# V tiles of the cross-attention moved from ahead of the loop into slots 0 to 7, Wo split in slots 1 and 3, one context buffer

## The chip, the cores and the metric

The kernel runs on one core of a Trainium2 chip. The metric is the device time of one execution in microseconds. The core has TensorE (PE in the profile), VectorE (DVE), ScalarE (ACT), GpSimd (POOL) and SyncE (SP); each runs its own instructions in order, and they wait for each other through semaphores. DMAs are issued by an engine's queue (mostly SyncE's, some ScalarE's).

## The reference

Multi-head cross-attention of 16 batches with 512 query rows of 512 features against 77 context rows, 16 heads of 32 features, followed by a residual and a layer norm:

```python
Q = split_heads(query @ Wq + bq)          # query: (16, 512, 512)
K = split_heads(key @ Wk + bk)            # key = value = context: (16, 77, 512)
V = split_heads(value @ Wv + bv)
scores = jnp.einsum('bhqd,bhkd->bhqk', Q, K) / np.sqrt(D_K).astype(np.float32)
attn = jax.nn.softmax(scores, axis=-1)
ctx = jnp.einsum('bhqk,bhkd->bhqd', attn, V)
ctx = ctx.transpose(0, 2, 1, 3).reshape(B, S, D_MODEL)
out = ctx @ Wo + bo
return _layer_norm(out + query, ln_gamma, ln_beta)
```

## The kernel before

Products with a weight matrix are made of three matmuls each, because both operands are split into a high and a low part: high x high, high x low, low x high. A product over 512 features is thus 4 x 3 = 12 matmuls.

**Stage one, `project_context`.** The context of all batches is 1232 columns. For each chunk of 128 features ScalarE casts Wk and the context to their high parts and VectorE subtracts to get the low parts; the context is cut in two pieces, `cx1` (the first `V_FIRST * P` = 512 columns) and `cx2` (720 columns, which lie in the tail of the buffers `ch` and `cl` that the loop uses later for the context of the attention). TensorE makes K in 12 tiles (four chunks of output features, each cut at columns 0, 512, 872 and 1232), ScalarE and VectorE evict it as high and low part, and SyncE stores it to DRAM in four pairs of DMAs. Then TensorE makes the first four V tiles (128 context rows each, from `cx1`) in the banks `pvv`, VectorE adds bv, and SyncE stores them. SyncE's order is: the K stores, a wait for them to land, four loads of `kb` (K of batch 0 laid out for the maxima), then the V stores, each behind a wait for VectorE. All engines meet at the end of the stage.

**Stage two, `attend`.** A loop over 64 chunks (16 batches x 4 groups of four heads), one per slot; the first 16 slots and the last ones are written out, the rest is a hardware loop. Lags set which work of which chunk falls in a slot. In slot g TensorE does, in this order: the Q product of chunk g (`p_q`, 12 matmuls); in slots 0 to 5 one of the six remaining V tiles (`project_v` into `p_o`); from slot 4 on the values (`p_v`) and sums (`p_den`) of chunk g-4; from slot 3 on the first two score matmuls (`p_s`) of chunk g-3; and then four times a quarter of the output projection (from slot 8 on, `p_o`), a score matmul at two of these, and one `p_a` matmul, whose rows VectorE reduces to maxima. `p_a` has two banks, so the third and fourth wait for VectorE's first and second maxima. The score matmuls need `z`, which SyncE's queue puts together for a pair of slots: eight copies of the high part of Q, four of the low part, and four of the negated maxima (`z<-nmt`), in the second slot of a pair and at the start of the next.

VectorE does in slot g: the sums over keys of chunk g-4 (`sum_keys`), later slots' residual (`add_residual`), the low part of Q (`q_low`), the inverse of the sums and the division (`divide`, into one of two buffers of `cxt`), and the four maxima; in slots 0 to 5 the addition of bv to a V tile (`add_bv`) stands between the second and the third maximum. ScalarE then casts `cxt` to `ch`, and GpSimd subtracts to get `cl`.

Wo is split to `woh` and `wol` in slots 6 and 7; these lie where Wv's parts were, so the names `woh` and `wol` in rows of V tiles mean Wv. Its raw chunks lie in `xn` and in two buffers of `y`. The rows of gamma, beta and bo are loaded in slot 6.

Of the kernel before, what the change touches and what calls it, by code (L numbers as in the profile page):

```python
# [20 lines left out]
F32 = mybir.dt.float32  # L21
# [26 lines left out]
WO_SLOTS = (6, 7)  # L48

V_FIRST = 4  # L50
V_SLOTS = (0, 1, 2, 3, 4, 5)
# [37 lines left out]
def v_tiles(B, S2):  # L89

    return [(r, min(P, B * S2 - r)) for r in range(0, B * S2, P)]


def v_products(nc, keep, bank, parts, r, m):

    (cxh, cxl), wvh, wvl = parts, keep["wvh"], keep["wvl"]
    for kc in range(KC):
        for n, (x, w) in enumerate(((cxh, wvh), (cxh, wvl), (cxl, wvh))):
            last = nc.tensor.matmul(bank[0:m, :], x[:, kc, r:r + m], w[:, kc, :],  # L99
                                    start=(kc == 0 and n == 0), stop=(kc == KC - 1 and n == 2))  # L100
    return last


def project_context(nc, a, keep, kh_dram, kl_dram, v_dram, B, S2):
# [4 lines left out]
    cuts = [0, N1, N1 + (NK - N1) // 4 * 2, NK]  # L109
# [7 lines left out]
    with ExitStack() as ctx:  # L117
# [3 lines left out]
        def sem(name):  # L121
# [25 lines left out]
            (cx[:, kc % CX, N1:NK], cx2[0][:, kc, :], cx2[1][:, kc, :]))]  # L147
# [3 lines left out]
        with nc.Block() as block:  # L151
# [143 lines left out]
            @block.tensor  # L295
            def _(pe):
                def k_products(i, kc):
                    c, lo, hi = tiles_k[i]
                    (cxh, cxl), at = (cx1, lo) if hi <= N1 else (cx2, lo - N1)
                    for n, (w, x) in enumerate(((wkh, cxh), (wkh, cxl), (wkl, cxh))):  # L300
                        last = nc.tensor.matmul(pk[i % PK][:, 0:hi - lo], w[:, kc, P * c:P * (c + 1)],
                                                x[:, kc, at:at + hi - lo],
                                                start=(kc == 0 and n == 0), stop=(kc == KC - 1 and n == 2))
                    if kc == KC - 1:
                        last.then_inc(k_summed, 1)


                for kc in range(KC):
                    for i in range(PK):
                        if i < 2:  # L310
                            pe.wait_ge(kv_low, 3 * kc + 2 + i)
                        k_products(i, kc)
                for i in range(PK, 2 * PK):
                    pe.wait_ge(k_low_out, i - PK + 1)
                    for kc in range(KC):
                        k_products(i, kc)
                pe.wait_ge(kv_low, 4 * KC)
                for i, (r, m) in enumerate(tiles_v):
                    if i >= 2:
                        pe.wait_ge(v_out, i - 1)  # L320
                    v_products(nc, keep, pv[i % 2], cx1, r, m).then_inc(v_summed, 1)


def attend(nc, a, keep, kh_dram, kl_dram, v_dram, out, B, S, S2):
# [17 lines left out]
    assert VT <= V_FIRST + len(V_SLOTS) and max(V_SLOTS) < LAG_PV + 2  # L342
# [3 lines left out]
    with ExitStack() as ctx:  # L346
# [89 lines left out]
        def v_in_slot(g):  # L436

            if not isinstance(g.u, int):
                return []
            return [V_FIRST + n for n, k in enumerate(V_SLOTS[:VT - V_FIRST]) if k == PAIR * g.u + g.k]  # L440
# [8 lines left out]
        p_vp = p_o  # L449
        wo_raw = [xn[:, 0, :], xn[:, 1, :], y[:, 2, :], y[:, 3, :]]  # L450
# [18 lines left out]
        def _(sp):  # L469
# [56 lines left out]
            def slot(g):  # L526
# [20 lines left out]
                if g.back(WO_SLOTS[0] - 1).is_first():  # L547
                    load_wo(2)
                    load_wo(3)
# [19 lines left out]
        def _(pe):  # L569
# [97 lines left out]
            def project_v(i):  # L667

                pe.wait_ge(v_out, i)
                r, n = tiles_v[i]  # L670
                v_products(nc, keep, p_vp[:], keep["cx2"], r - V_FIRST * P, n).then_inc(v_summed, 1)

            def slot(g):
# [4 lines left out]
                for i in v_in_slot(g):  # L678
                    project_v(i)
# [26 lines left out]
        def _(act):  # L706
# [25 lines left out]
            def ctx_high(g):  # L732
                i = g.k // NCH % 2
                act.wait_ge(cx_ready, g.over(1, 1))
                if g.back(2).is_first():
                    act.wait_ge(v_summed, VT)
                if g.k % NCH == 0:
                    at_least(act, o_summed, g.over(NCH, -1, QT))
                nc.scalar.copy(ch[:, i, g.k % NCH, :], cx[:, g.k % 2, :]).then_inc(ch_ready, 1)  # L739
# [8 lines left out]
            def load_residual(m):  # L748

                if m.is_first():  # L750
                    act.wait_ge(wo_low, 2)
                    act.wait_ge(wo_high, 2)
# [29 lines left out]
            def split_wo_high(kc):  # L782
                act.wait_ge(wo_in[kc % 2], 16 * (kc // 2 + 1))
                act.wait_ge(v_summed, VT)
                nc.scalar.copy(keep["woh"][:, kc, :], wo_raw[kc]).then_inc(wo_high, 1)
# [3 lines left out]
            def slot(g):  # L789
# [30 lines left out]
                for i in v_in_slot(g):  # L820
                    store_v(i)
                if g.back(WO_SLOTS[0]).is_first():
# [33 lines left out]
        def _(dve):  # L856
# [6 lines left out]
            def add_residual(m):  # L863
# [3 lines left out]
                at_least(dve, stored[i], m.over(4, 0, 16))  # L867
                nc.vector.scalar_tensor_tensor(out=y[:, i, :], in0=p_o[:], scalar=0.0, in1=xn[:, m.k % 2, :],
# [56 lines left out]
            def add_bv(i):  # L925
# [4 lines left out]
                nc.vector.tensor_tensor(y[0:n, i % 4, :], p_vp[0:n, :], bv_row[0:n, :],  # L930
# [9 lines left out]
            def slot(g):  # L940
# [16 lines left out]
                if g.valid(NG):  # L957
                    for t in range(QT):
                        row_maxima(g, t)
                        if t == 1:  # L960
                            for i in v_in_slot(g):
                                add_bv(i)
# [69 lines left out]
        def _(pool):  # L1032
# [42 lines left out]
            def slot(g):  # L1075
# [56 lines left out]
def xattn(nc, a, out):  # L1132
# [5 lines left out]
    with ExitStack() as ctx:  # L1138

        keep = {n: ctx.enter_context(nc.sbuf_tensor(n, [P, KC, D], F32R)) for n in ("wqh", "wql", "woh", "wol")}  # L1140
# [46 lines left out]
```

## Time and profile before

| | us |
|---|---|
| median of 3 runs | 627.71 |
| lowest and highest run | 625.75, 628.01 |
| the profiled execution, its whole time | 627.87 |
| the profiled execution, span of the instructions | 626.0 |

| engine | busy us in the span |
|---|---|
| TensorE | 598.1 |
| VectorE | 496.7 |
| GpSimd | 444.9 |
| ScalarE | 363.6 |

The span is what the trace shows, from the first to the last instruction; the profiled execution's own time is 1.87 us more. Times in rows are counted from the span's start. Slot 0 begins at 48.75 us, slot 9 at 121.01 us. Matmuls are pipelined: the busy time of one is longer than the distance from its start to the next one's start, and the distance is what a stream of them costs.

### The profile page before, as it was taken

The page shows a single profiled execution, that of the slowest core. Times are in us where ns is not written, and L with a number is a line of the kernel's source. Part 1 is how long each engine was busy: PE and PEld are TensorE (multiplying, and loading weights), DVE is VectorE, ACT ScalarE, POOL GpSimd, SP SyncE. Part 2 cuts the span into 40 slices and gives each one's busy share as a digit, 9 for nine tenths or more (in the row PEclk, how much of TensorE's full clock was granted, in tenths as well). Part 3 has the DMA queues.
Part 4 walks back from the last instruction along what each step waited for, and adds up shares of the span by engine and source line. Part 5 has one row for each costly group of instructions (what it writes and reads, how often), then busy time and mean ns, then how long its engine had stood idle before and what let it go on. Part 6 is the DMA issues. An engine that isn't in the chain of part 4 may idle for free.

```text
span 626.0 us, 12033 instructions
## 1 busy us (share of the span) xinstructions
PE 598.1 (96%) x3336; PEld 432.3 (69%) x3336; DVE 496.7 (79%) x912; ACT 363.6 (58%) x675; POOL 444.9 (71%) x396
## 2 busy tenths in 40 slices
PE   5998999999999999999999999999999999999793
PEld 5986765677777777777777777777777777776362
DVE  5423478888888888888888988888888888888575
ACT  5621235566666666666666666666666666656362
POOL 1335024648888888888888888888888888878676
PEclk9999999999999999999999999999999999999797
DMA  8757778988979898989898979989797989796413
GB/s 313 292 225 190 193 183 222 205 186 200 231 197 228 212 223 209 206 218 218 211 216 207 231 201 219 219 202 245 177 241 198 231 204 233 190 225 169 122 52 134
DMA packets 93392, 129.58 MB, mean 207 GB/s; under 512 B 49936, under 2 KB 49936, under 8 KB 93360
## 3 DMA queue, kind: packets, MB, share of 16 engines
q1 hardware_dynamic: 74544, 94.94, 60.9%
q10 hardware_dynamic: 18816, 34.25, 21.3%
q8 instruction: 15, 0.25, 0.2%
q14 instruction: 17, 0.14, 0.1%
HBM read 53.94 MB, written 24.35 MB: 125 GB/s over the span
## 4 chain that ended last, share of the span: by engine, by line
PE 83%; POOL 2%; DVE 2%; SPq 2%; issue 1%; ACT 1%; DMA 0%; POOLq 0%; ACTq 0%; DVEq 0%
PE p_q L579 29%; PE p_o L645 25%; PE p_s L609 10%; PE p_v L620 10%; PE p_a L595 6%; PE p_o L99 3%; SPq L523 1%; DVE nm L921 1%; PE p_den L628 1%; DMA z<-nmt 0%; DVE rden L886 0%; ACT prob L714 0%; POOL cl L1062 0%; POOL xt L1104 0%; POOL y L1053 0%
## 5 line engine op out<-in xcount | busy, mean ns | idle before, releaser
L714 ACT ACTIVATE prob<-p_s 77x512 f32<-77x512 f32 x256 | 143.2, 591 | 108.2 <-PE p_s L609 93.0
L1062 POOL TENSOR_TENSOR cl<-cxt,ch 128x512 fp32r<-128x512 f32 x64 | 83.1, 1298 | 115.0 <-ACT ch L739 115.0
L921 DVE TENSOR_REDUCE nm<-p_a 128x4 f32<-128x308 f32 x256 | 115.9, 475 | 49.3 <-PE p_a L595 48.1
L876 DVE TRANSPOSE_TENSOR_REDUCE part<-prob 96x64 f32<-96x2048 f32 x64 | 146.4, 2287 | 2.4 <-issue 1.3
L729 ACT ACTIVATE qh<-p_q,bq_col 128x512 fp32r<-128x512 f32 x64 | 44.0, 687 | 125.0 <-PE p_q L579 125.0
L579 PE MATMUL p_q<-xh,wqh 128*128 128x512 f32 x256 | 101.1, 395 | 1.7 <-PEq L151 1.7
L579 PE MATMUL p_q<-xl,wqh 128*128 128x512 f32 x256 | 101.3, 396 | 0.0
L579 PE MATMUL p_q<-xh,wql 128*128 128x512 f32 x256 | 101.0, 395 | 0.0
L609 PE MATMUL p_s<-z,ks 97*77 97x512 f32 x256 | 95.8, 415 | 5.2 <-DMA z<-nmt 3.7
L645 PE MATMUL p_o<-woh,ch 128*128 128x512 f32 x240 | 96.0, 400 | 0.8 <-issue 0.7
L645 PE MATMUL p_o<-wol,ch 128*128 128x512 f32 x240 | 95.1, 396 | 0.0
L645 PE MATMUL p_o<-woh,cl 128*128 128x512 f32 x240 | 94.6, 394 | 0.0
L1043 POOL TENSOR_TENSOR xl<-xt,xh 128x512 fp32r<-128x512 f32 x60 | 77.2, 1287 | 20.0 <-ACT xh L721 19.9
L595 PE MATMUL p_a<-kb,qh 128*128 128x308 f32 x256 | 79.1, 312 | 2.9 <-DVE nm L921 2.8
L1057 POOL TENSOR_TENSOR y<-y,beta_row 128x512 f32<-128x512 f32 x58 | 75.2, 1297 | 4.5
L1069 POOL TENSOR_TENSOR xn<-xn,bo_row 128x512 f32<-128x512 f32 x60 | 77.3, 1289 | 0.0
L1053 POOL TENSOR_TENSOR y<-y,gamma_row 128x512 f32<-128x512 f32 x58 | 74.4, 1283 | 0.0
L620 PE MATMUL p_v<-prob,vb 77*32 77x512 f32 x512 | 69.1, 612 | 0.0
L595 PEld LDWEIGHTS p_a<-kb,qh 128*128 128x128 f32 x256 | 48.3, 189 | 22.9 <-DVE nm L921 7.6
L913 DVE SCALAR_TENSOR_TENSOR ql<-p_q,bq_col,qh 128x512 fp32r<-128x512 f32 x64 | 47.9, 748 | 17.0 <-ACT qh L729 13.5
L645 PEld LDWEIGHTS p_o<-woh,ch 128*128 128x128 f32 x240 | 45.6, 190 | 18.2 <-issue 5.5
L579 PEld LDWEIGHTS p_q<-xh,wqh 128*128 128x128 f32 x256 | 48.1, 188 | 13.2 <-issue 2.1
(127 smaller groups left out, 934.4 us busy)
## 6 DMA issues: line engine op xcount, KB each, us to landing
z<-qh SPq DMA_DIRECT2D x256, 128.0 KB, 3.7
z<-ql SPq DMA_DIRECT2D x128, 128.0 KB, 4.8
xn<-in_x ACTq DMA_DIRECT2D x60, 256.0 KB, 3.3
out_dram<-y SPq DMA_DIRECT2D x60, 256.0 KB, 4.3
xt<-in_x_t ACTq DMA_DIRECT2D x58, 256.0 KB, 4.9
ks<-k_high SPq DMA_DIRECT2D x32, 154.0 KB, 4.7
cx<-in_ctx_t SPq DMA_DIRECT2D x4, 616.0 KB, 5.6
k_high<-kth SPq DMA_DIRECT2D x4, 616.0 KB, 3.4
```

Source lines behind the costliest of these rows:

```text
L579: last = nc.tensor.matmul(p_q[:], w[:, kc, P * c:P * (c + 1)], x[:, i, kc, :], start=(kc == 0 and n == 0), stop=(kc == KC - 1 and n == 2))
L595: nc.tensor.matmul(p_a[t % 2][:, 0:HC * S2], qh[:, g.k // 2 % 2, g.k % 2, P * t:P * (t + 1)], kb[g.k // NCH % 2][:, g.k % NCH, :], start=T ...
L609: nc.tensor.matmul(p_s[j % 2][0:S2, :], ks[0:KR, g.k // NCH % 2, h, :], z[0:KR, i, j, g.k % 2, :], start=True, stop=True).then_inc(s_summe ...
L620: nc.tensor.matmul(p_v[DK * j:DK * (j + 1), :], vb[0:S2, g.k // NCH % 2, DK * h:DK * (h + 1)], prob[0:S2, j, :], start=True, stop=True)
L645: last = nc.tensor.matmul(p_o[:], x[:, i, kc, P * t:P * (t + 1)], w[:, kc, :], start=(kc == 0 and n == 0), stop=(kc == KC - 1 and n == 2))
L714: nc.scalar.activation(prob[0:S2, j, :], p_s[j % 2][0:S2, :], ACT.Exp, scale=SCALE).then_inc(prob_ready, 1)
L876: nc.vector.tensor_reduce(part[:], prob[0:KP, :, :].rearrange("p h (i r) -> p (h i) r", r=DK), AX_X, ALU.add, apply_transpose=True).then_i ...
L921: nc.vector.tensor_reduce(nm[:, t, g.k % 2:HALF:2], p_a[t % 2][:, 0:HC * S2].rearrange("p (h k) -> p h k", k=S2), AX_X, ALU.max, negate=Tr ...
L1043: nc.gpsimd.tensor_tensor(xl[:, i, n.k % KC, :], xt[:, n.k % 2, :], xh[:, i, n.k % KC, :].bitcast(F32), ALU.subtract).then_inc(xl_ready, 1)
L1057: nc.gpsimd.tensor_tensor(rows(m), rows(m), beta[:], ALU.add).then_inc(y_done, 1)
L1062: nc.gpsimd.tensor_tensor(cl[:, i, g.k % NCH, :], cx[:, g.k % 2, :], ch[:, i, g.k % NCH, :].bitcast(F32), ALU.subtract).then_inc(cl_ready, 1)
L1069: nc.gpsimd.tensor_tensor(xn[:, m.k % 2, :], xn[:, m.k % 2, :], bo[:], ALU.add).then_inc(xb_ready, 1)
```

## The change

Ahead of the loop there are two V tiles instead of four (`V_FIRST`). The other 976 context rows are cut into eight tiles of 122 rows, one for each of the slots 0 to 7, and their 12 matmuls are no longer in one piece behind the Q product: a quarter (three matmuls) stands ahead of each `p_a` matmul, as the output projection does from slot 8 on. The sums over keys therefore stand right behind the Q product. The addition of bv moves to the next slot, ahead of `q_low` on VectorE, and so does the V tile's store on ScalarE's queue. The second piece of the context, now 976 columns, lies tile by tile (8 x 4 x 122) instead of chunk by chunk, so the K matmuls on it read four runs of 122 columns; K is cut at columns 0, 256, 744 and 1232. Wv's parts have buffers of their own, so Wo can be split early, in slots 1 and 3, through `xn` alone; SyncE's queue waits for the first half's split before it loads the second. The rows of gamma, beta and bo are loaded in slot 5. `cxt` has one buffer, so a division waits until the last one's result is split. Two unused buffers go, and the scratch for dynamic DMAs is made smaller.

```diff
-WO_SLOTS = (6, 7)
+WO_SLOTS = (1, 3)
+ROWS_SLOT = 5
-V_FIRST = 4
-V_SLOTS = (0, 1, 2, 3, 4, 5)
+V_FIRST = 2
+V_LATE = 8
...
-    return [(r, min(P, B * S2 - r)) for r in range(0, B * S2, P)]
+    first = V_FIRST * P
+    width = (B * S2 - first) // V_LATE
+    return [(P * i, P) for i in range(V_FIRST)] + [(first + width * k, width) for k in range(V_LATE)]
...
-    cuts = [0, N1, N1 + (NK - N1) // 4 * 2, NK]
+    cuts = [0, N1, (N1 + NK) // 2, NK]
...
-            (cx[:, kc % CX, N1:NK], cx2[0][:, kc, :], cx2[1][:, kc, :]))]
+            (cx[:, kc % CX, N1:NK].rearrange("p (k n) -> p k n", k=V_LATE), cx2[0][:, :, kc, :], cx2[1][:, :, kc, :]))]
...
-                    (cxh, cxl), at = (cx1, lo) if hi <= N1 else (cx2, lo - N1)
+                    bank = pk[i % PK][:, 0:hi - lo]
+                    if hi <= N1:
+                        cxh, cxl = (t[:, kc, :] for t in cx1)
+                    else:
+                        half = V_LATE // 2
+                        k = half * (lo > N1)
+                        cxh, cxl = (t[:, k:k + half, kc, :] for t in cx2)
+                        bank = bank.rearrange("p (k n) -> p k n", k=half)
...
                 if kc >= 2:
-                    sp.wait_ge(v_stored[kc], 32)
-                sp.dma_start(wo_raw[kc], a["Wo"][P * kc:P * (kc + 1), :]).then_inc(wo_in[kc % 2], 16)
+                    sp.wait_ge(wo_high, kc - 1)
+                    sp.wait_ge(wo_low, kc - 1)
+                sp.dma_start(xn[:, kc % 2, :], a["Wo"][P * kc:P * (kc + 1), :]).then_inc(wo_in[kc % 2], 16)
...
-                for i in v_in_slot(g):
-                    project_v(i)
                 if v.valid(NG) and g.valid(NG):
                     values(v)
                     sums(v)
...
                     if o.valid(NS):
                         project_out(o, kc)
+                    for i in v_in_slot(g):
+                        project_v(i, kc)
                     if s.valid(NG) and g.valid(NG) and kc in (1, 2):
                         scores(s, kc + 1)
...
-                at_least(dve, ch_ready, g.over(1, -1))
-                at_least(dve, cl_ready, g.over(1, -1))
-                nc.vector.tensor_tensor(cx[:, i, :], p_v[:], rden[:], ALU.mult).then_inc(cx_ready, 1)
+                at_least(dve, ch_ready, g.over(1))
+                at_least(dve, cl_ready, g.over(1))
+                nc.vector.tensor_tensor(cx[:], p_v[:], rden[:], ALU.mult).then_inc(cx_ready, 1)
...
+                for i in v_in_slot(g.back(1)):
+                    add_bv(i)
                 if m.valid(NS) and g.valid(NG):
                     add_residual(m)
...
-                        if t == 1:
-                            for i in v_in_slot(g):
-                                add_bv(i)
...
-        keep["wvh"], keep["wvl"] = keep["woh"], keep["wol"]
...
-    nc = bacc.Bacc("TRN2", target_bir_lowering=False, num_devices=1)
+    nc = bacc.Bacc("TRN2", target_bir_lowering=False, num_devices=1, dynamic_dma_scratch_size=2048)
```

On TensorE, at the end of slot 0, before (`p_o` rows are V matmuls, `p_a` rows feed the maxima, `p_q` rows are the Q product):

```order
L99 MATMUL p_o<-woh,ch 128x512
L99 MATMUL p_o<-wol,ch 128x512
L99 MATMUL p_o<-woh,cl 128x512
L595 MATMUL p_a<-kb,qh 128x308 x4
L579 MATMUL p_q<-xh,wqh 128x512
```

The same engine in slot 0 of the changed kernel, from the end of the Q product:

```order
L587 MATMUL p_q<-xh,wql 128x512
L102 MATMUL p_o<-wvh,ch 122x512
L102 MATMUL p_o<-wvl,ch 122x512
L102 MATMUL p_o<-wvh,cl 122x512
L603 MATMUL p_a<-kb,qh 128x308
L102 MATMUL p_o<-wvh,ch 122x512
```

The four `p_a` stood together behind the whole V tile; now each stands behind a quarter of it.

On TensorE in slot 4, before, from the last V matmul on, with what each waits for (`p_v` the values, `p_den` the sums, `p_s` the scores):

```order
L99 MATMUL p_o<-woh,cl 128x512
L620 MATMUL p_v<-prob,vb 32x512 [waits vb_in0,prob_ready]
L620 MATMUL p_v<-prob,vb 32x512 x3
L628 MATMUL p_den<-part,sel 32x16 [waits part_ready]
L628 MATMUL p_den<-part,sel 32x16 x3
L609 MATMUL p_s<-z,ks 77x512 [waits prob_ready,mx_in0,z_in0]
```

The same place in the changed kernel, from the last matmul of the Q product on:

```order
L587 MATMUL p_q<-xh,wql 128x512
L628 MATMUL p_v<-prob,vb 32x512 [waits vb_in0,prob_ready]
L628 MATMUL p_v<-prob,vb 32x512 x3
L636 MATMUL p_den<-part,sel 32x16 [waits part_ready]
L636 MATMUL p_den<-part,sel 32x16 x3
L617 MATMUL p_s<-z,ks 77x512 [waits prob_ready,mx_in0,z_in0]
L617 MATMUL p_s<-z,ks 77x512 [waits prob_ready]
L102 MATMUL p_o<-wvh,ch 122x512 [waits v_out]
```

The V tile stood ahead of the sums, and now stands behind the first two score matmuls; it waits for the bank `p_o` (`v_out`), which VectorE frees in the same slot.

On SyncE's queue, around slot 2, before (`z` for slots 0 and 1, then V of batch 0, then `z` for slots 2 and 3):

```order
L523 DMA z<-ql 32x1024 x3
L518 DMA z<-nmt 1x32x32 [waits max_turned]
L518 DMA z<-nmt 1x32x32 x3
L493 DMA vb<-v_all 77x512 [waits v_stored0]
L523 DMA z<-qh 32x1024 [waits qh_ready]
```

The same place in the changed kernel:

```order
L531 DMA z<-ql 32x1024 x3
L526 DMA z<-nmt 1x32x32 [waits max_turned]
L526 DMA z<-nmt 1x32x32 x3
L500 DMA vb<-v_all 77x512 [waits v_stored0]
L515 DMA xn<-in_Wo 128x512 [waits wo_low,wo_high] x2
L531 DMA z<-qh 32x1024 [waits qh_ready]
```

The second half of Wo, with its wait for ScalarE and GpSimd, now stands ahead of the `z` copies of slots 2 and 3.

## Rows read from the trace of the kernel before

**Rows 1.** The page, chain that ended last: share of the span by engine

```profile
PE 83%; POOL 2%; DVE 2%; SPq 2%; issue 1%; ACT 1%; DMA 0%; POOLq 0%; ACTq 0%; DVEq 0%
```

**Rows 2.** Windows, slots 0, 3, 4, 6, 9: length, busy per engine, granted clock, DMA

```profile
core 0: us, PE busy (x) PEld busy (x) DVE busy (x) ACT busy (x) POOL busy (x), PEclk, DMA share, GB/s
48.75:55.91 7.16, 6.72 (x28) 5.22 (x29) 1.98 (x5) 1.72 (x3) 6.96 (x5) 1.00 0.99 237
...
70.07:78.14 8.07, 7.68 (x33) 5.57 (x33) 3.08 (x7) 2.68 (x5) 0.00 (x0) 1.00 0.54 137
78.14:87.82 9.68, 9.14 (x49) 5.98 (x49) 7.05 (x12) 3.76 (x8) 1.29 (x1) 1.00 0.78 188
...
97.46:104.64 7.18, 6.34 (x38) 3.72 (x37) 6.84 (x12) 4.16 (x9) 2.55 (x2) 1.00 0.82 216
...
121.01:129.29 8.28, 8.28 (x50) 6.01 (x49) 7.00 (x12) 4.69 (x10) 3.79 (x3) 1.00 1.02 188
```

**Rows 3.** Timeline of slot 0: start, duration, engine, instruction, idle before and releaser

```profile
51.63 0.39 PE L99 MATMUL p_o<-woh,ch 128*128 128x512 f32 x1
...
51.88 0.69 ACT L729 ACTIVATE qh<-p_q,bq_col 128x512 fp32r<-128x512 f32 x1 [14.38 <-PE p_q L579]
...
54.41 0.45 PE L595 MATMUL p_a<-kb,qh 128*128 128x308 f32 x2
...
55.28 0.80 PE L595 MATMUL p_a<-kb,qh 128*128 128x308 f32 x2 [0.43 <-DVE nm L921]
```

**Rows 4.** Timeline of SyncE's queue at the end of stage one

```profile
37.56 0.43 SPq L184 DMA_DIRECT2D k_low<-ktl  x1
41.63 1.77 SPq L193 DMA_DIRECT2D kb<-k_high  x4
43.44 0.90 SPq L197 DMA_DIRECT2D v_all<-y  x2
...
47.83 0.33 SPq L197 DMA_DIRECT2D v_all<-y  x1
```

**Rows 5.** Timeline of TensorE: first V matmul of stage one, first matmul of stage two

```profile
35.71 0.40 PE L99 MATMUL pvv<-woh,cx1h 128*128 128x512 f32 x1
...
48.75 0.47 PE L579 MATMUL p_q<-xh,wqh 128*128 128x512 f32 x1 [1.69 <-PEq L151]
```

**Rows 6.** Timeline of TensorE: two K matmuls of 360 columns

```profile
31.76 0.33 PE L301 MATMUL pk<-ch,wkh 128*128 128x360 f32 x1
31.93 0.33 PE L301 MATMUL pk<-cl,wkh 128*128 128x360 f32 x1
```

**Rows 7.** Timeline of the first context chunk's casts and its second subtraction

```profile
5.00 0.62 ACT L203 CAST cx1h<-cx 128x512 fp32r<-128x512 f32 x1 [0.96 <-DMA cx<-in_ctx_t]
5.53 0.79 ACT L203 CAST ch<-cx 128x720 fp32r<-128x720 f32 x1
...
6.35 0.91 DVE L244 TENSOR_TENSOR cl<-cx,ch 128x720 fp32r<-128x720 f32 x1
```

**Rows 8.** Windows in the tail, columns as in rows 2

```profile
587.00:591.00 4.00, 4.00 (x13) 1.41 (x13) 1.70 (x2) 0.00 (x0) 3.92 (x4) 0.50 0.00 0
591.00:592.00 1.00, 1.00 (x4) 0.69 (x3) 0.00 (x0) 0.00 (x0) 0.71 (x1) 0.55 0.65 246
```

**Rows 9.** Timeline of TensorE in the tail: the first matmuls after a gap

```profile
586.77 1.11 PE L609 MATMUL p_s<-z,ks 97*77 97x512 f32 x2 [3.69 <-DMA z<-nmt]
```

**Rows 10.** Timeline of SyncE's queue: z for slots 0 and 1

```profile
59.62 5.42 SPq L523 DMA_DIRECT2D z<-qh  x8
...
67.63 3.20 SPq L518 DMA_DIRECT2D z<-nmt  x4
```

**Rows 11.** Tile z, 50 to 110 us: from issue to landing

```profile
DMA to landing us min/median/max: 2.3/3.3/4.7
```

**Rows 12.** Timeline in the tail: GpSimd's subtraction and VectorE's next division

```profile
603.94 1.28 POOL L1062 TENSOR_TENSOR cl<-cxt,ch 128x512 fp32r<-128x512 f32 x1 [1.78 <-ACT ch L739]
...
608.07 0.69 DVE L906 TENSOR_TENSOR cxt<-p_v,rden 128x512 f32<-128x512 f32 x1
```

More of the change, by code:

```diff
@@ L89, in v_tiles, with v_products @@
 def v_tiles(B, S2):
-    return [(r, min(P, B * S2 - r)) for r in range(0, B * S2, P)]
[L94 to L100, printed above, removed]
+    first = V_FIRST * P
+    width = (B * S2 - first) // V_LATE
+    assert width <= P and first + V_LATE * width == B * S2
+    return [(P * i, P) for i in range(V_FIRST)] + [(first + width * k, width) for k in range(V_LATE)]
+def v_products(nc, keep, bank, cxh, cxl, kc, m):
+    wvh, wvl = keep["wvh"], keep["wvl"]
+    for n, (x, w) in enumerate(((cxh, wvh), (cxh, wvl), (cxl, wvh))):
+        last = nc.tensor.matmul(bank[0:m, :], x, w[:, kc, :],
+                                start=(kc == 0 and n == 0), stop=(kc == KC - 1 and n == 2))
     return last
@@ L320, in _ @@
                         pe.wait_ge(v_out, i - 1)
-                    v_products(nc, keep, pv[i % 2], cx1, r, m).then_inc(v_summed, 1)
+                    for kc in range(KC):
+                        cxh, cxl = (t[:, kc, r:r + m] for t in cx1)
+                        last = v_products(nc, keep, pv[i % 2], cxh, cxl, kc, m)
+                    last.then_inc(v_summed, 1)
 def attend(nc, a, keep, kh_dram, kl_dram, v_dram, out, B, S, S2):
@@ L439, in v_in_slot @@
                 return []
-            return [V_FIRST + n for n, k in enumerate(V_SLOTS[:VT - V_FIRST]) if k == PAIR * g.u + g.k]
+            return [V_FIRST + n for n in range(V_LATE) if n == PAIR * g.u + g.k]
         def wo_in_slot(g):
@@ L546, in slot @@
                     store(g.back(LAG_STORE))
-                if g.back(WO_SLOTS[0] - 1).is_first():
+                if g.back(WO_SLOTS[0] + 1).is_first():
                     load_wo(2)
@@ L665, in project_last, with project_v @@
                         last.then_inc(o_summed, 1)
[L667 to L671, printed above, removed]
+            def project_v(i, kc):
+                if kc == 0:
+                    pe.wait_ge(v_out, i)
+                m = tiles_v[i][1]
+                cxh, cxl = (t[:, i - V_FIRST, kc, :] for t in keep["cx2"])
+                last = v_products(nc, keep, p_o, cxh, cxl, kc, m)
+                if kc == KC - 1:
+                    last.then_inc(v_summed, 1)
             def slot(g):
@@ L734, in ctx_high @@
                 act.wait_ge(cx_ready, g.over(1, 1))
-                if g.back(2).is_first():
-                    act.wait_ge(v_summed, VT)
+                if isinstance(g.u, int) and PAIR * g.u + g.k < V_LATE:
+                    act.wait_ge(v_summed, V_FIRST + PAIR * g.u + g.k + 1)
                 if g.k % NCH == 0:
                     at_least(act, o_summed, g.over(NCH, -1, QT))
-                nc.scalar.copy(ch[:, i, g.k % NCH, :], cx[:, g.k % 2, :]).then_inc(ch_ready, 1)
+                nc.scalar.copy(ch[:, i, g.k % NCH, :], cx[:]).then_inc(ch_ready, 1)
             def square(m):
@@ L750, in load_residual @@
                 if m.is_first():
[L751 to L752 removed]
+                    act.wait_ge(wo_low, KC)
+                    act.wait_ge(wo_high, KC)
                 all_at_least(act, (squared, m.over(1, -1)))
@@ L867, in add_residual @@
                 at_least(dve, stored[i], m.over(4, 0, 16))
+                if isinstance(m.u, int) and PAIR * m.u + m.k < 4:
+                    dve.wait_ge(v_stored[i], 16 * len(tiles_v[i::4]))
                 nc.vector.scalar_tensor_tensor(out=y[:, i, :], in0=p_o[:], scalar=0.0, in1=xn[:, m.k % 2, :],
@@ L947, in slot @@
                     minus_mean_over_std(g.back(LAG_NORMALIZE))
+                for i in v_in_slot(g.back(1)):
+                    add_bv(i)
                 if m.valid(NS) and g.valid(NG):
@@ L1149, in xattn @@
             keep[n] = ctx.enter_context(nc.sbuf_tensor(n, shape, dt))
-        keep["wvh"], keep["wvl"] = keep["woh"], keep["wol"]
         n2, part = B * S2 - V_FIRST * P, 2 * KC * S
-        assert KC * n2 <= part - 2 * S
+        assert KC * n2 <= part
         for n in ("ch", "cl"):
@@ L1156, in xattn @@
             keep[n] = buffer[:].rearrange("p (b c s) -> p b c s", b=2, c=KC)
-            keep.setdefault("cx2", []).append(buffer[:, part - KC * n2:part].rearrange("p (c n) -> p c n", c=KC))
+            late = buffer[:, part - KC * n2:part]
+            keep.setdefault("cx2", []).append(late.rearrange("p (k c n) -> p k c n", k=V_LATE, c=KC))
         for n in ("bq_in", "xh_ready", "xl_ready", "kb0_zeroed", "v_summed", "v_out"):
```

24 lines of the change are left out of this document (8 added, 16 removed).

## The prediction

> **What bounds the kernel now.** I read the chain of work that ended last first: TensorE (PE) carries 83% of it [rows 1], so what counts is when TensorE works, and whether it works without a break. The windows by slot come next, since the change touches slots 0 to 8 and the stage ahead of them [rows 2]. The reader is to see three kinds of slot. From slot 9 on TensorE is busy for all of its 8.28 us. Slot 0 takes 7.16 us with 0.44 idle, and slots 0 to 2 have 21.3 together (48.75 to 70.07). Slot 4 takes 9.68, with 0.54 idle and VectorE busy for 7.05, and slot 5 the same (87.82 to 97.46); both have a V tile ahead of the sums that VectorE's chain waits for. Slot 6, which has no V tile, takes 7.18, of which VectorE works 6.84. From the first row's 48.75 to the last row's 121.01 slots 0 to 8 take 72.26 us. Last I read the seam between the two stages: SyncE's queue and TensorE around 36 to 49 us [rows 4, 5].
>
> **Two V tiles fewer ahead of the loop.** A V tile is 12 matmuls, 2.78 us (51.63 to 54.41) [rows 3], so two tiles less are 5.6 us of TensorE. Not all of that comes off, because SyncE's queue is next late. Before, it sends the last K rows at 37.56, waits until they have landed, sends the four kb loads from 41.63, two V stores from 43.44 for 0.90, and the last V store at 47.83, for which it had waited [rows 4]; the loop's first matmul stands 0.59 after that store's end (48.16 to 48.75) [rows 4, 5]. With two stores the queue is through at 44.34, and slot 0 starts at 44.93 if K ends as before. K ends a little later, for two reasons. The context is cut at 256 instead of 512 columns, so the second piece has 976 instead of 720: VectorE's subtraction of it, 0.91 us before, becomes about 1.23 [rows 7], and TensorE's first tile is half as long and no longer covers it. That is worth between 0 and 0.9 (the whole row); I take 0.4. And the last K tile has 488 instead of 360 columns: at the casts' slope (0.62 for 512, 0.79 for 720 columns) and VectorE's 0.91 for 720 [rows 7] its two evictions grow by 0.10 and 0.16. Slot 0 starts at 44.93 + 0.40 + 0.25 = 45.6: **3.2 us** gained.
>
> **The K matmuls** themselves have as many columns as before. Spacing is 0.23 for 512 (2.78 / 12 [rows 3]) and 0.17 for 360 [rows 6], so it falls with the columns, and 256 would be 0.12. No row shows a matmul so short behind a 128-column weight load; if the load could not go under the 0.17 that the rows show, 48 of them would cost 48 x 0.045 = 2.1 us. I take 0, as the spacing shows no floor yet. The Trainium skill (TensorE: Matmul & The Clock Gate, section LDWEIGHTS) has a weight load take its columns at 1.2 GHz, an estimate of 107 ns for 128 columns: by that the term is 0 too, by the row's bound 2.1; no row here shows the load alone.
>
> **The idle seam.** TensorE has its last V matmul out at 35.71 + 0.4 + 24 x 0.233 = 41.7 and drained 0.17 later (0.40 less 0.23) [rows 5], and waits until 45.6: 3.7 us instead of 1.69. The trace has both. After 1.69 the granted clock is 1.00 and the first 12 matmuls take 2.88 (48.75 to 51.63), full spacing [rows 2, 3, 5]. In the tail a gap of 3.69 ends at 586.77 [rows 9]; the granted clock behind it is 0.50 (1.2 of 2.4 GHz) from 587 to 591 and has a mean of 0.55 in 591 to 592 [rows 8], so it is back at 591.9: 5.1 us of work at half speed, which loses up to 2.5 us. So the price is between 0 and 2.5. I take **1.7**: the gap is as long as the tail's, but dense matmuls stand before and after it, where the tail's were broken. The Trainium skill (the same page, section Why this matters for your kernels) warns that idle gaps between bursts of matmuls throw the clock back; by that rule the sum is the one below, by the row of 1.69 it is 1.7 less, and the tail's gap agrees with the rule.
>
> **Slots 0 to 2** have the V tile in four parts between the four p_a matmuls, instead of ahead of them. p_a needs qh, ready at 51.88 + 0.69 = 52.57, 0.94 after the Q product's stream ends at 51.63 [rows 3]; the first 0.70 of V covers most of that, and about 0.35 stays. The wait of 0.43 for VectorE's maxima [rows 3] goes, since 0.70 of V lies between any two p_a. A slot is 2.80 + 2.78 + 0.35 + 4 x 0.15 = 6.53; three with a slow first matmul 19.7 against 21.3.
>
> **Slot 3** is where part of it goes back. Its score matmuls stand ahead of V now and need z, which SyncE's queue fills: it starts at 59.62, 3.7 after slot 1's beginning (48.75 + 7.16 = 55.91 [rows 2]), and its last copy goes out at about 70.1, 10.5 later [rows 10]; landing is 2.3 to 4.7, median 3.3 [rows 11]. Counted from slot 0's start, now: 6.6 + 3.7 + 10.5 + 3.3 = 24.1, while the Q product ends at 19.7 + 2.8 = 22.5. So a wait of 1.6 (0.6 to 3.0) that V hid before, and a slot of 2.80 + 1.6 + 4 scores of 0.23 + 2.78 + 0.6 = 8.7 instead of 8.07 [rows 2].
>
> **Slots 4 to 8** each have the work of slot 9: a V tile is as many matmuls as an output projection, and VectorE's addition of bv takes the place of the residual's. The sums stand right behind the Q product in slots 4 and 5, so VectorE's chain no longer starts a V tile late. I take 8.28 for each [rows 2]. Slots 4 and 5 gain 1.4 each, slot 6 pays 1.1 for its new tile, and 7 and 8 together (104.64 to 121.01 before) pay 0.2. In all 19.7 + 8.7 + 5 x 8.28 = 69.8 against 72.26: **2.5 us** gained.
>
> **Edits at nothing.** One context buffer: VectorE's next division now waits for GpSimd's subtraction; the tightest place is the tail, where it ended at 603.94 + 1.28 = 605.22 and the division began at 608.07 [rows 12], 2.85 to spare; gone, it would delay the maxima behind it on VectorE, and TensorE's p_a with them. Wo in slots 1 and 3: four ScalarE casts (0.62 for this width [rows 7]) and four GpSimd subtractions (1.28 [rows 12]) move to slots in which both engines have most of their time free [rows 2]; SyncE's wait for the first two stands behind the z copies and the V load of slot 2, ahead of slot 3's z, which cannot go before slot 3's qh anyway. If that cover fails, slot 3's z is late by as much, but it is not needed until slot 5. The row constants go out a slot sooner on ScalarE's queue, the extra weight buffers cost memory only, and the smaller scratch belongs to no queue that the trace shows.
>
> **Sum.** The profiled execution took 627.87 (span 626.0), 0.16 above the median of 627.71. 627.87 - 3.2 - 2.5 + 1.7 = **623.9**.
>
> **Rivals.** (a) The clock holds over the seam, as it did over 1.69: 622.2. For it: the work around is dense; against: the tail. (b) z lands late in slot 3: 4.7 instead of 3.3 makes the wait 3.0, close to the tail's gap, so that the clock may fall a second time: 623.9 + 1.4 = 625.3, and with 2.5 more 627.8; half of that gives 626.6. For it: the stores of V and the loads of x share these microseconds; against: the median landing. (c) Slower than before: the K matmuls on the second context piece now read four separate runs of 122 columns instead of 360 in a row. There are 96, all ahead of the seam, so that every delay is the total's. From 4.0 / 96 = 0.042 us each, a fifth of their 0.22 (0.23 x 488 / 512), the gain is gone; at 0.08 each, 7.7 in all, the time is 631.6. No row shows such a read, and none shows a cost for one; the K stage has no other cover. (d) That the two tiles leave the stage and it does not end sooner is priced above: 3.2 instead of 5.6.
>
> **How the numbers follow.** The forecast has a chance of 0.47, (a) 0.25, (b) 0.20, (c) 0.08. A measurement of this kernel tells about 0.5%, 3.1 us, from no change, so faster ends at 624.6. All of (a) and 0.33 of the forecast lie below: faster 0.58; the rest of the forecast and (b) make 0.34; slower is (c). The range goes from (a) with an early landing, 622.2 - 0.9 = 621.3, to (b)'s upper end, 627.8.
>
> **What would show it.** The first Q product at 45.6, not 48.75, after an idle gap of 3.7; a granted clock of 0.5 behind it, or the Q product at full spacing if (a); slots 0 to 2 at 6.5 at full clock; in slot 3 a wait for z of about 1.6; slots 4 to 8 at 8.3. I am wrong if the stage ahead of the loop ends later than 46.5, if a slot from 4 to 8 takes over 8.6, or if a slot after 9 differs from 8.28.

## The result, and the profile after

The changed kernel is slower: 639.73 us (637.77 to 640.92) against 627.27 (625.75 to 628.01), a ratio of 1.0208 with an interval of 1.0187 to 1.0229. The prediction was 623.9, with a range that ended at 627.8. The profiled execution took 640.92, its span 639.1, which is 13.1 more than before. The chain that ended last, as in [rows 1]:

```profile
PE 80%; DMA 4%; SPq 4%; POOL 2%; issue 1%; ACT 1%; DVE 0%; POOLq 0%; ACTq 0%; DVEq 0%
```

DMA had 0% before and has 4% now.

Windows of the changed kernel by slot, columns as in [rows 2]: slots 0, 1, 3, slots 4 to 8 together, slot 9.

```profile
core 0: us, PE busy (x) PEld busy (x) DVE busy (x) ACT busy (x) POOL busy (x), PEclk, DMA share, GB/s
46.17:54.33 8.16, 8.03 (x28) 6.17 (x29) 2.16 (x5) 1.72 (x3) 7.03 (x5) 0.79 1.05 243
54.33:60.83 6.50, 6.41 (x31) 4.95 (x29) 3.17 (x6) 2.23 (x4) 2.62 (x3) 1.00 0.41 100
67.31:84.73 17.42, 10.13 (x34) 7.58 (x33) 3.27 (x6) 3.17 (x6) 0.00 (x0) 0.71 0.79 173
84.73:126.17 41.44, 41.44 (x242) 29.86 (x241) 35.29 (x53) 20.40 (x37) 13.99 (x11) 1.00 0.77 189
126.17:142.60 16.43, 11.21 (x50) 7.92 (x49) 7.03 (x12) 4.94 (x10) 5.02 (x4) 0.79 0.84 187
```

Two slots stick out. Slot 3 takes 17.42 where 8.7 was forecast (8.07 before [rows 2]), and slot 9, which the change was not to touch, 16.43 instead of 8.28. Slots 4 to 8 take 41.44, that is 8.29 each, slot 1 6.50: as forecast. What TensorE waited for from slot 0 to slot 10 (columns: total, times, longest):

```profile
PE p_s L617 <- DMA z<-nmt: 7.3, 1, 7.3
PE p_o L653 <- DVE y L881: 5.0, 1, 5.0
PE p_q L587 <- PEq L154: 3.8, 1, 3.8
```

Three waits, one in each of slots 3, 9 and 0. The last is the seam that the prediction spoke of. **Slot 9's wait**, followed back in the chain of work that ended last (start, duration, what), and VectorE's timeline there:

```profile
118.01 17.15 DMA v_all<-y
...
135.29 0.15 DVE y L881
```

```profile
135.29 0.69 DVE L881 SCALAR_TENSOR_TENSOR y<-p_o,xn 128x512 f32<-128x512 f32 x1 [6.23 <-DMA v_all<-y]
```

The store of slot 6's V tile, the last but one, went out at 118.01 and landed 17.15 us later. VectorE's residual (`add_residual`, L880) has a new wait for that store, because its result goes into the same buffer of `y`; the description of the change does not name this wait. VectorE stood 6.23 us, and TensorE 5.02 behind it.

**Slot 3's wait** is for `z`. SyncE's queue for slots 0 and 1, as in [rows 10], and from issue to landing for tile z, 50 to 110 us, as in [rows 11]:

```profile
58.05 8.63 SPq L531 DMA_DIRECT2D z<-qh  x8
...
70.27 3.03 SPq L526 DMA_DIRECT2D z<-nmt  x4
```

```profile
DMA to landing us min/median/max: 2.8/5.0/8.1
```

The same eight copies took 8.63 us to issue instead of 5.42, and landing took up to 8.1 instead of 4.7 (for the copies of Q; the view gives no landing of `z<-nmt`). Nothing in the change touches these copies. Both slots pay twice, since TensorE's clock fell behind each wait; windows of the changed kernel in slot 0, slot 3 and slot 9:

```profile
47.00:49.00 2.00, 2.00 (x6) 1.57 (x5) 0.00 (x0) 0.00 (x0) 1.94 (x2) 0.50 0.87 276
78.00:82.00 4.00, 4.00 (x12) 3.06 (x11) 0.48 (x1) 1.13 (x3) 0.00 (x0) 0.50 1.04 171
135.00:140.00 5.00, 3.95 (x10) 3.21 (x11) 3.42 (x9) 1.12 (x3) 1.28 (x1) 0.51 0.97 238
```

The granted clock (the column ahead of the DMA share) is 0.50 or 0.51, the lower level of 1.2 instead of 2.4 GHz, in all three. Set the two slots to what was forecast for them, and the profile gives 640.92 - (17.42 - 8.7) - (16.43 - 8.28) = 624.05. So the rest of the sum held, and the question is why a V store takes 17 us and z's copies are late.

### The profile page after: what moved, and what is told of

Same layout as the page of the kernel before. It is cut to its first block, busy times and chain, and to the rows that moved or that the text cites. A ratio compares the mean times of both kernels' runs of the same rounds, so it can differ in the third digit from the quotient of the medians.

```text
span 639.1 us, 12041 instructions
## 1 busy us (share of the span) xinstructions
PE 601.9 (94%) x3336; PEld 436.7 (68%) x3336; DVE 497.9 (78%) x912; ACT 364.6 (57%) x675; POOL 444.6 (70%) x396
## 4 chain that ended last, share of the span: by engine, by line
PE 80%; DMA 4%; SPq 4%; POOL 2%; issue 1%; ACT 1%; DVE 0%; POOLq 0%; ACTq 0%; DVEq 0%
PE p_q L587 27%; PE p_o L653 25%; PE p_s L617 10%; PE p_v L628 9%; PE p_a L603 5%; SPq L531 3%; DMA v_all<-y 3%; PE p_o L102 3%; DMA z<-nmt 1%; SPq L526 1%; PE p_den L636 1%; POOL cl L1074 0%; POOL y L1065 0%; POOL xt L1116 0%; ACT prob L726 0%
## 5 line engine op out<-in xcount | busy, mean ns | idle before, releaser
L934 DVE TENSOR_REDUCE nm<-p_a 128x4 f32<-128x308 f32 x256 | 117.4, 476 | 62.8 <-PE p_a L603 61.8
```

The source lines that it names most:

```text
L934: nc.vector.tensor_reduce(nm[:, t, g.k % 2:HALF:2], p_a[t % 2][:, 0:HC * S2].rearrange("p (h k) -> p h k", k=S2), AX_X, ALU.max, negate=Tr ...
```

## The experiments

The theory (A) was the shape of the store: 122 rows instead of 128. The rivals were (B) that the V stores, now in the same microseconds as z's copies, crowd them out whatever their shape, and (C) that the loads of the row constants, which went out at 101.4 to 102.6 ahead of the last stores on ScalarE's queue, hold them back.

**e1: the same bytes in other pieces.** Each late V tile is stored as 112 and 10 rows; the semaphore counts follow.

```diff
-                act.dma_start(v_dram...[r:r + n, :], y[0:n, i % 4, :]).then_inc(v_stored[i % 4], 16)
+                for lo, hi in ((0, 112), (112, 122)):
+                    act.dma_start(v_dram...[r + lo:r + hi, :], y[lo:hi, i % 4, :]).then_inc(v_stored[i % 4], 16)
```

> The changed kernel with each store of a late V tile sent as two DMAs, of 112 and of 10 rows, instead of one of 122. Theory A: a DMA of 122 rows is spread over few of the 16 DMA engines, so it lands late (17 us in the trace) and whatever else goes through those engines queues behind it. Then slot 3's wait for z falls from 7.3 to about 1.6 us, slot 9's wait for the V store goes, slots 3 and 9 take 8.7 and 8.3, and the time is about 624. Rival B: the shorter slots 0 to 2 crowd the transfers of V, x, Wo and z into less time. Bytes and times are unchanged here, so both waits stay and the time is 638 to 641. Rival C: the V stores wait behind the three row loads on ScalarE's queue, moved to slot 5. Then slot 9's wait stays, some 6 us with a fall of the clock behind it, and only slot 3 could change.

Measured: 624.64 (ten runs, 622.94 to 626.14) against 626.47, ratio 0.9964 (0.9949 to 0.9979). TensorE's waits over the same stretch, SyncE's queue for slots 0 and 1, and the windows of slots 0 and 3:

```profile
PE p_q L593 <- PEq L160: 3.8, 1, 3.8
PE p_s L623 <- DMA z<-nmt: 1.0, 1, 1.0
PE p_s L623 <- issue: 0.3, 1, 0.3
```

```profile
58.16 5.64 SPq L537 DMA_DIRECT2D z<-qh  x8
```

```profile
45.40:54.44 9.04, 9.04 (x28) 7.07 (x29) 2.13 (x5) 1.72 (x3) 6.99 (x5) 0.67 0.93 219
67.42:75.72 8.30, 7.25 (x34) 5.55 (x33) 3.26 (x6) 3.14 (x6) 0.00 (x0) 1.00 0.70 175
```

The wait for the store is gone, z's first eight copies take 5.64 to issue, slot 3 takes 8.30 and slot 9 8.28. The bytes, the queue and the moment are the same, with one DMA more, so (B) and (C) fall. Landing of z's copies of Q over the whole stretch is hardly shorter, though:

```profile
DMA to landing us min/median/max: 2.6/4.4/7.5
```

So the 8.1 above is no mark of the 122 rows; it belongs to a copy that went out at 103.67, long after slot 3's. What slot 3 waits for is the last `z<-nmt` copy of slots 0 and 1. The trace also keeps the times at which a DMA steps its semaphore, its sign of landing, which the views do not print. By these steps that copy went out at 72.62 and landed at 77.31 in the changed kernel, and at 69.34 and 71.18 here: 3.3 later out and 2.9 longer under way.

**e2: is it the splitting or the row count?** Two pieces again, of 61 rows each: `((0, 61), (61, 122))` in e1's line.

> The same with two DMAs of 61 and 61 rows: as many DMAs as with 112 and 10, the same bytes. Theory A, if it is the number of rows that decides how many engines share a DMA: 61 has no divisor up to 16, so the stores land no sooner than with 122 rows and perhaps twice as late; the waits in slots 3 and 9 are 7 us or more each and the time is 640 or above, up to 670. If it was only that one DMA was split in two, the time is that of 112 and 10 rows, about 624. Rivals B and C: 638 to 641, as for one DMA.

Measured: 673.48 in one execution. One store on ScalarE's queue, the second piece of a tile, and TensorE's waits from 45 to 200 us:

```profile
65.43 7.33 ACTq L798 DMA_DIRECT2D v_all<-y  x1
```

```profile
PE p_a L609 <- ACT qh L747: 21.5, 3, 12.2
PE p_o L659 <- DVE y L888: 11.6, 2, 6.4
PE p_s L623 <- DMA z<-nmt: 4.0, 1, 4.0
PE p_q L593 <- PEq L160: 3.8, 1, 3.8
```

Smaller pieces are not the cure. That store keeps the queue for 7.33 us, so that ScalarE comes late to `qh`; with the stores of later tiles, TensorE waits 21.5 for `qh` in all. Bytes and number of DMAs are those of e1, so what counts is the number of rows in a piece. The Trainium skill (DMA: Bandwidth & Descriptors, section Why a DMA increments its semaphore by 16 and not by 1, on how many engines) says that a transfer is given to as many of the 16 DMA engines as the largest number up to 16 that divides its rows: 16 for 112 or 128, 10 for 10, but 2 for 122 and 1 for 61, always the first ones. The trace agrees on how many. A store of 128 rows steps its semaphore 16 times as it lands (kernel before). Each store of 122 rows steps it twice, besides one step at its issue (at 133.31 and 135.16 for the one that slot 9 waited for), and each of 61 rows once; the two pieces of e1 together make 16 and 10. No row shows which engines worked. By the last steps, the stores of the loop landed in 9.7 to 18.0 us in the changed kernel, in 4.0 to 8.0 in e1 (both pieces) and in 2.2 to 4.4 before.

**e9: one such store with nothing beside it.** The kernel before, with the last output rows of all stored as 122 and 6 rows.

```diff
-                sp.dma_start(out_dram[NS + t], x_last[t]).then_inc(stored[t], 16)
+                for lo, hi in (((0, 122), (122, P)) if t == 1 else ((0, P),)):
+                    sp.dma_start(out_dram[NS + t][lo:hi, :], x_last[t][lo:hi, :]).then_inc(stored[t], 16)
```

> The kernel before, where the very last store of the output (128 rows of 512) is sent as 122 and 6 rows; nothing else is on the queues by then, and the kernel ends when it has landed. Theory A: a store of 122 rows is slow by itself; the time rises by what it lands later, 6 to 14 us. If it was slow only because it stood behind others: no more than 1 us.

Measured: 633.19 (two runs), ratio 1.0110 (1.0077 to 1.0142), span 631.5. The last store on SyncE's queue, before and then here:

```profile
623.54 0.33 SPq L564 DMA_DIRECT2D out_dram<-xt  x1
```

```profile
623.26 0.69 SPq L565 DMA_DIRECT2D out_dram<-xt  x2
```

Before, the span ends 2.5 us after that row begins (626.0 - 623.5); here 8.2 (631.5 - 623.3). So a 122-row store is 5.7 us slower with nothing beside it but the other 6 rows, a little under the 6 to 14 expected. Windows with stores of 128 rows before, and behind the 122 rows here, columns as in [rows 2]:

```profile
622.00:624.00 2.00, 0.00 (x0) 0.00 (x0) 1.03 (x2) 0.00 (x0) 0.79 (x1) 0.50 1.01 378
```

```profile
626.00:630.00 4.00, 0.00 (x0) 0.00 (x0) 0.00 (x0) 0.00 (x0) 0.00 (x0) 0.50 0.12 44
```

The mean busy share of the 16 DMA engines is 0.12, what two busy ones of 16 give (0.125), and they move 44 GB/s instead of 378. So few engines are the cause of the slow store, as theory A has it. The 17.15 of the changed kernel is twice its 8.2; what adds the rest was not separated.

**e3: the shape alone in the kernel before.** The five loop tiles of 128 rows are stored as 122 and 6 rows, in the old order of work.

```diff
+    return ((0, 122), (122, n)) if i >= V_FIRST and n == P else ((0, n),)
...
-                act.dma_start(v_dram...[r:r + n, :], y[0:n, i % 4, :]).then_inc(v_stored[i % 4], 16)
+                for lo, hi in v_pieces(i, n):
+                    act.dma_start(v_dram...[r + lo:r + hi, :], y[lo:hi, i % 4, :]).then_inc(v_stored[i % 4], 16)
```

> The kernel before, where only the five stores of 128 rows in slots 0 to 4 are cut into 122 and 6 rows. Theory A: the V stores land in over 10 us instead of 2 to 4, the z copies of slots 0 to 3 are held up, TensorE waits for z in slot 3 or 5, and the time rises by 3 to 12 us. Rival B: the slots are as long as before, so nothing changes but one more DMA to issue per slot: 626 to 628.5.

Measured: 630.36 (629.55 to 636.22), ratio 1.0078 (1.0047 to 1.0108). TensorE's longest wait for scores (in slot 7), the clock behind it, and ScalarE's queue:

```profile
PE p_s L619 <- issue: 2.6, 1, 2.6
```

```profile
114.00:115.00 1.00, 1.00 (x4) 0.61 (x3) 0.80 (x2) 0.91 (x3) 0.00 (x0) 0.50 0.90 188
```

```profile
69.96 3.23 ACTq L790 DMA_DIRECT2D v_all<-y  x2
78.76 5.32 ACTq L790 DMA_DIRECT2D v_all<-y  x2
```

The stores of 122 and 6 rows landed in 9.3 to 17.8 us by their semaphore steps, as expected. The view names no releaser for the wait of 2.6, but it was for z, too: the last step of `z<-nmt` came at 111.73, 0.07 before the weight load of these scores (111.80). Behind it the granted clock fell to 0.50. The cost is 4.9 us (0.0078 x 626), not the 16.9 that slots 3 and 9 of the changed kernel had over their forecast. In the old order V stands ahead of the scores and covers z in slot 3, and `add_residual` does not wait for a store; but there are also five such stores here instead of eight. That 122 rows need the new order of work to cost what they did is likely, not shown.

**e4: the seam.** e1, with 14 matmuls whose result nobody reads between the last V tile of stage one and the loop.

```diff
                     last.then_inc(v_summed, 1)
+                pe.wait_ge(v_out, 1)
+                r, m = tiles_v[1]
+                for again in range(14):
+                    nc.tensor.matmul(pv[0][0:m, :], cx1[0][:, again % KC, r:r + m], wvh[:, again % KC, :], start=True, stop=True)
```

> The changed kernel with stores of 112 and 10 rows, and 14 matmuls behind the last V tile of stage one whose result nothing reads: they fill the seam ahead of the loop, in which TensorE was idle for 3.8 us. If it is the idle time that brings the clock down: the first Q product takes 2.8 to 2.9 us instead of 4.6 to 5.5, slot 0 6.6, and the time falls by 1.6 to 2.5, to about 622.5. If the slow start belongs to the start of a stage, whatever TensorE did before: slot 0 stays at 8 to 9 us and the time at 624.6.

Measured: 622.14 (620.66 to 624.10) against 626.04, ratio 0.9935 (0.9914 to 0.9955). The loop's first matmul, and the windows of slots 0, 3 and 4 (slot 5 is like slot 4):

```profile
45.64 0.47 PE L598 MATMUL p_q<-xh,wqh 128*128 128x512 f32 x1 [0.61 <-PEq L160]
```

```profile
45.64:52.30 6.66, 6.51 (x28) 5.03 (x29) 2.16 (x5) 1.72 (x3) 6.46 (x5) 1.00 1.06 268
65.29:73.83 8.54, 7.25 (x35) 5.54 (x33) 3.26 (x6) 3.14 (x6) 0.00 (x0) 1.00 0.70 181
73.83:82.11 8.28, 8.28 (x51) 5.96 (x49) 7.14 (x11) 4.59 (x9) 3.79 (x3) 1.00 0.99 212
```

The gap is 0.61 instead of 3.8, the clock stays at 1.00, and slot 0 takes 6.66 instead of 8.16 (changed kernel) or 9.04 (e1): the idle time was the cause of the low clock. This version has the lowest median here, ahead of both kernels.

**e6: slot 3 without its wait.** e4, with two quarters of V and their `p_a` ahead of the first scores in slot 3.

```diff
+                ahead = 2 if s.is_first() else 0
+                for kc in range(ahead):
+                    for i in v_in_slot(g):
+                        project_v(i, kc)
+                    rowmax_scores(g, kc)
                 if s.valid(NG):
                     scores(s, 0)
```

> The same, and in slot 3 alone the first two quarters of the V tile, each with its p_a matmul, stand ahead of the first score matmuls, which wait for z. If the wait of 1.1 us for z that is left in slot 3 is one that a V tile can hide, as it did before: slot 3 takes 7.2 to 7.5 instead of 8.3 and the time falls by another 0.8 to 1.1, to about 621.5. If VectorE's maxima, which now come sooner, or z itself only shift the wait: no difference, 622.5.

Measured: 622.86 (620.33 to 624.38) against 626.04, ratio 0.9941 (0.9924 to 0.9959), no gain over e4. The windows of slots 3 to 5, and ScalarE in slots 3 and 4:

```profile
65.69:73.81 8.12, 7.58 (x34) 5.50 (x33) 3.17 (x6) 3.14 (x6) 0.00 (x0) 1.00 0.61 162
73.81:83.33 9.52, 8.80 (x51) 5.81 (x49) 7.12 (x11) 5.25 (x10) 4.12 (x4) 1.00 1.03 189
83.33:92.18 8.85, 8.34 (x50) 5.96 (x49) 6.97 (x10) 3.33 (x7) 2.27 (x2) 1.00 1.07 237
```

```profile
77.74 0.62 ACT L814 CAST woh<-xn 128x512 fp32r<-128x512 f32 x1 [1.19 <-DMA xn<-in_Wo]
...
78.71 0.69 ACT L758 ACTIVATE qh<-p_q,bq_col 128x512 fp32r<-128x512 f32 x1 [0.34 <-issue]
```

Slot 3 gained 0.42, but slots 4 and 5 lost 1.8. ScalarE waited for Wo's second half to land, and `qh` of slot 4 came behind it. That made Wo's casts the suspect.

**e10: Wo's second half one slot later.** e6 with `WO_SLOTS = (1, 4)` for `(1, 3)`.

> The version with warm matmuls and slot 3's early maxima, and one number more: Wo's second half is cast in slot 4 instead of slot 3. In the run before, ScalarE waited 1.81 and 1.19 us in slot 3 for Wo's second half to land, the second cast began at 77.74, and qh of slot 4 came only at 78.71; slot 4 took 9.52 and slot 5 8.85 instead of 8.28 to 8.30 each. Theory (these casts hold up qh, and through it slots 4 and 5): no cast waits in slot 3, slots 4 and 5 together take 16.6 to 17.2 instead of 18.37, and the profiled time falls by 1.2 to 1.8 against the version before, to about 621 (ratio to the kernel before 0.990 to 0.993). Rival (slots 4 and 5 are long because slot 3 is short: z or VectorE's chain is late whatever ScalarE does): slots 4 and 5 together stay at 18.0 to 18.5 and the time at 622.9.

Measured: 624.06 (620.48 to 625.90) against 627.24, ratio 0.9945 (0.9921 to 0.9969). Windows of slots 3 to 5, and TensorE's wait in slot 5:

```profile
66.14:74.26 8.12, 7.58 (x35) 5.50 (x34) 3.17 (x6) 3.15 (x6) 0.00 (x0) 1.00 0.63 173
74.26:82.53 8.27, 8.27 (x50) 5.96 (x49) 7.14 (x11) 3.44 (x7) 1.30 (x1) 1.00 1.05 221
82.53:92.61 10.08, 8.35 (x51) 5.97 (x49) 7.02 (x10) 5.05 (x10) 5.01 (x4) 1.00 1.09 193
```

```profile
88.27 0.66 PE L628 MATMUL p_s<-z,ks 97*77 97x512 f32 x2 [1.73 <-issue]
```

The theory was half right. Slot 4 is back to 8.27, so the casts had held it up; but slot 5 now takes 10.08, and slots 4 and 5 together 18.35, as the rival had it. Slot 5's first scores need z of slots 2 and 3, whose last copies went out at 81.9. The row names no releaser, but the semaphore of `z<-nmt` made its last step at 88.18, 0.06 before the weight load of these scores (88.24). In e6 it was 87.75 and 87.81; in e4 the last step came at 85.41, TensorE at 86.04, and there was no wait. So it is z that holds slot 5. SyncE's queue began those copies 24.5 us after slot 0 here and 24.4 in e4 (70.98 - 46.49, 70.04 - 45.64), so they do not move when slot 3 gets shorter, and slot 5 meets them.

**e7: V in one piece.** e1 with each late V tile whole behind the Q product, as the kernel before had it.

```diff
+                for i in v_in_slot(g):
+                    for kc in range(KC):
+                        project_v(i, kc)
...
-                    for i in v_in_slot(g):
-                        project_v(i, kc)
```

> The changed kernel with stores of 112 and 10 rows, but each late V tile in one piece right behind the Q product, as before. If the gain of the slots comes from the V matmuls among the maxima and behind the sums: slots 0 to 2 go back to 7.1, slots 4 to 7 to 9.6 each, slot 3 loses its wait for z; 3 x 0.6 + 4 x 1.35 - 1.1 = 6 us more, about 630.5. If only the matmuls' number counts: 624.6.

Measured: 633.67 in one execution. Of TensorE's waits from 45 to 150 us, those for VectorE:

```profile
PE p_o L108 <- DVE y L951: 2.9, 4, 0.9
PE p_a L609 <- DVE nm L942: 2.3, 7, 0.4
```

Slots 1 and 2 take 7.11 and 7.12 instead of 6.50, and slots 4 to 7 between 10.48 and 10.83 instead of 8.3. Eight tiles in one piece cost 9 us over the same tiles among the maxima (633.67 - 624.64). Of these, 2.9 are the waits for `y` in slots 4 to 7, which belong to this mixture alone: the addition of bv frees the bank `p_o` only in the next slot, where the V tile now comes first. The kernel before has no such wait. The other 6 are what was expected of V's place among the maxima and behind the sums.

**e11: one context buffer.** The kernel before with `cxt` of one buffer.

```diff
-        cx = sb("cxt", [P, 2, S], F32)
+        cx = sb("cxt", [P, S], F32)
...
-                at_least(dve, ch_ready, g.over(1, -1))
-                at_least(dve, cl_ready, g.over(1, -1))
+                at_least(dve, ch_ready, g.over(1))
+                at_least(dve, cl_ready, g.over(1))
```

> The kernel before with one buffer of cxt instead of two and nothing else: VectorE's division waits for GpSimd's subtraction of the division before. Theory (the prediction's edit at nothing): a division at 300.6, its subtraction ended by 304.9, the next division 8.28 after the first, so about 4 us to spare in the steady slots and 2.85 at the tightest place in the tail: no slot differs by over 0.05, ratio 1.000 within 0.002. Rival: slots 5 to 8, where VectorE is busy for 7 of its microseconds, or the tail lose a few tenths each: 1 to 3 us in all, ratio 1.002 to 1.005.

Measured: 627.07 against 627.24, ratio 0.9999 (0.9982 to 1.0016). The interval leaves room for 1 us, but the slots begin within 0.05 of where they did (slot 7 at 104.69 instead of 104.64): the buffer costs nothing there.

## Why the prediction was wrong

**The step that failed** is the one on slots 0 to 8, with what it left out among the edits at nothing. It said that slots 0 to 8 gain 2.5, and priced the V tiles by TensorE's and VectorE's work alone. Two things were put at nothing without a reason. The sum has no term for the store of a late V tile, whose shape went from 128 to 122 rows; it landed in up to 18.0 us instead of 4.4 and held up z, which cost 8.72 in slot 3 (17.42 - 8.7). And `add_residual` had been given a wait for that store, which no step named: 8.15 in slot 9 (16.43 - 8.28). Together these are 16.9 of the 17.0 by which the profiled execution missed the forecast (640.92 - 623.9).

**Slot 3's wait** was named, placed and priced (1.6, at most 3.0 by landing [rows 11]), but [rows 10, 11] were taken beside stores of 128 rows, and [rows 11] has no landing of the `z<-nmt` copies, which come last (2.7 by their semaphore, 70.15 to 72.89). Beside stores of 122 rows the wait was 7.29, and the clock fell as rival (b) had it. With 112 and 10 rows it was 1.0 and slot 3 took 8.30: the step's size was right for the transfers that it assumed. Rival (b) had the mechanism, z late and the clock down, yet its price came from the same rows.

**Stage one** was forecast to end 3.2 sooner, at 45.6. It ended at 46.17 in the changed kernel and at 45.40 in e1, which has the same stage, so 45.6 lies between two executions. SyncE's queue sends its last V stores a little after kb, as forecast:

```profile
42.86 1.77 SPq L196 DMA_DIRECT2D kb<-k_high  x4
44.67 0.90 SPq L200 DMA_DIRECT2D v_all<-y  x2
```

They stand 1.23 later than the same rows of [rows 4] (41.63 and 43.44), because K ends later (its last store 38.78 instead of 37.56); the two terms on K had allowed 0.65. In e1 they stand at 42.06 and 43.87, 0.43 later.

**The K matmuls** cost nothing. Those of 488 columns stand 0.225 apart, the 512-column spacing scaled:

```profile
35.13 0.39 PE L311 MATMUL pk<-ch,wkl 128*128 128x488 f32 x1
35.35 0.39 PE L311 MATMUL pk<-ch,wkh 128*128 128x488 f32 x1
```

Rival (c), strided reads, falls: the kernel did get slower, but for another reason. Those of 256 columns stand 0.12 apart (14.49, 14.60, 14.72), so the bound for a slow weight load does not bind either; by its own numbers it was 48 x 0.05 = 2.4, not 2.1.

**The idle seam** was right in size and kind: a gap of 3.80 (forecast 3.7), a clock of 0.50 behind it, and 8.16 - 6.50 = 1.66 lost (forecast 1.7). That 1.7 was a choice within a range, and e1, with the same gap, lost 2.5, the bound: the exact match is luck. e4 shows that the gap was the cause. Rival (a) falls.

**Slots 1, 2 and 4 to 8** were right: 6.50, 6.48 and 8.29 against 6.53 and 8.28. e7 shows that this comes from V's place among the maxima and behind the sums. **The edits at nothing:** one context buffer is nothing (e11). Wo in slot 3 is nothing in the changed kernel, where slot 4 took 8.27, but its casts decide slot 4 as soon as slot 3 is shorter (e6, e10).

With the store in 112 and 10 rows, the sum of the prediction is met in the trace: slot 9 begins at 117.50 instead of 121.01, 3.5 sooner, where 4.0 was forecast. The measured ratio, 0.9964, is a gain of 2.3 us (e1's executions span 622.94 to 626.14, and the trace is the first of these), so even then the change would have stood within the 0.5% that the prediction called no change. e4 adds what the seam had cost.

## What to carry to other kernels

When a tile's height changes, price its DMAs anew: bytes that hardly change say nothing, since stores of 122 rows landed here in 9.7 to 18.0 us, of 128 in 2.2 to 4.4 and of 112 and 10 in 4.0 to 8.0, and those of 122 held up transfers that had nothing to do with them. For each wait that a change adds, look up what it waits for and when that lands, a store's landing included. An idle stretch that cannot be taken away can be filled with matmuls that nobody reads, if the clock behind it falls.

## What the hardware showed that was not expected

- A store of 122 rows of 512 floats landed in 17.15 us among other transfers, and with nothing behind it the span ended 8.2 us after its issue began, against 2.5 for 128 rows, while the 16 DMA engines were busy 0.12 of the time; cut in 112 and 10 rows it made no wait.
- Its neighbours paid: eight copies on SyncE's queue took 8.63 us to issue instead of 5.42, though the V stores go out on ScalarE's; with 112 and 10 rows they took 5.64. A store of 61 rows kept ScalarE's own queue, and with it ScalarE, for up to 7.33 us.
- The granted clock fell to 0.50 after idle gaps of 2.60 (e3), 3.80, 5.02 and 7.29, and stayed at 1.00 after 0.61, 1.0, 1.69 [rows 5] and 1.73. The Trainium skill (TensorE: Matmul & The Clock Gate, section Why this matters for your kernels) warns of idle gaps between bursts of matmuls; these rows agree.
